# Stores of keys and values issued by ScalarE instead of SyncE, and an earlier first sample, in a two-layer cross-attention kernel on one core

## What is computed

```
x -> q = LN(x) Wq, k = LN(ctx) Wk, v = LN(ctx) Wv     16 heads of 8 columns
     rotary turn of q and k; scores = q k^T / sqrt(8) + bias(256 x 1601)
     att = softmax(scores) v;  x = x + gated projection;  x = x + tanh feed-forward
layer 2: q = LN(x) wq + bq, k = ctx wk + bk, v = ctx wv + bv, softmax(q k^T / sqrt(8)) v, wo
         then 8 experts with a top-2 gate, weighted sum
mask: all ones (looked at by the kernel, and a second program follows if it is not)
```

## Time and profile before

| | us |
|---|---|
| median of 3 runs | 655.69 (654.56 to 656.54) |
| the profiled execution | 653.17 |
| its span in the trace | 651.4 |
| PE busy | 561.3 (86% of the span) |
| ACT busy | 431.1 (66%) |
| DVE busy | 277.1 (43%) |
| POOL busy | 142.4 (22%) |

### The profile page before, as it was taken

The page is one execution under the profiler, slowest core; times in us unless marked ns, Lnnn a source line. Parts: engine busy times, 40 slices in busy tenths (PEclk is TensorE's granted clock), DMA queues, the critical chain, the costliest instruction groups (busy, mean ns, idle before and its releaser), DMA issues.

```text
span 651.4 us, 15145 instructions
## 1 busy us (share of the span) xinstructions
PE 561.3 (86%) x6326; PEld 278.2 (43%) x6326; DVE 277.1 (43%) x711; ACT 431.1 (66%) x486; POOL 142.4 (22%) x149
## 2 busy tenths in 40 slices
PE   4665896999979996999999999999999999999643
PEld 3432453545434553445555445434443443443231
DVE  5732742483754424544242243134344343433333
ACT  1224554866747773777778897998789869888400
POOL 5552622354436003541011000100000000000000
PEclk9867997999979997999999999999999999999856
DMA  6366264438755700445370066039016501000000
GB/s 166 94 186 178 71 218 168 104 115 243 226 157 146 264 26 5 138 130 179 83 189 28 27 147 141 27 82 230 4 46 144 133 10 53 2 1 10 1 0 12
DMA packets 54185, 68.12 MB, mean 105 GB/s; under 512 B 13347, under 2 KB 45551, under 8 KB 54112
## 3 DMA queue, kind: packets, MB, share of 16 engines
q1 hardware_dynamic: 50528, 59.29, 32.8%
q0 software_dynamic: 1280, 6.56, 3.4%
q10 hardware_dynamic: 2304, 1.25, 0.7%
HBM read 35.20 MB, written 18.83 MB: 83 GB/s over the span
## 4 chain that ended last, share of the span: by engine, by line
PE 53%; issue 14%; ACT 10%; SPq 7%; DMA 7%; DVE 7%; POOL 1%; ACTq 0%; POOLq 0%; DVEq 0%
PE ps L430 19%; PE ps L414 10%; ACT probs L941 8%; PE ps L408 7%; DMA k_scratch<-k_parts 4%; PE ps L360 4%; SPq L676 2%; PE ps L545 2%; SPq L699 1%; DMA ctx_tokens<-in_ctx 1%; PE ps L352 1%; PE ps L479 1%; PE ps L466 1%; DMA mask_q<-in_mask 1%; PE ps L472 1%
## 5 line engine op out<-in xcount | busy, mean ns | idle before, releaser
L941 ACT ACTIVATE probs<-ps 124x1024 f32<-124x1024 f32 (+1 forms) x416 | 399.8, 1024 | 110.7 <-PE ps L414 109.0
L430 PE MATMUL ps<-probs,values 124*9 124x256 f32 (+1 forms) x3328 | 221.4, 384 | 1.4 <-DVE out_sums L1268 1.3
L414 PE MATMUL ps<-q_side,k_side 63*124 63x256 bf16 (+1 forms) x1664 | 164.5, 283 | 13.0 <-ACT probs L941 11.2
L414 PEld LDWEIGHTS ps<-q_side,k_side 63*124 63x124 bf16 (+1 forms) x1664 | 98.1, 133 | 88.4 <-ACT probs L941 58.7
L430 PEld LDWEIGHTS ps<-probs,values 124*9 124x9 f32 (+1 forms) x3328 | 71.0, 90 | 94.1 <-issue 40.5
L408 PE MATMUL ps<-bias_g,bias_w 64*124 64x512 bf16 (+1 forms) x416 | 88.0, 419 | 25.5 <-ACT probs L941 22.0
L408 PEld LDWEIGHTS ps<-bias_g,bias_w 64*124 64x124 bf16 (+1 forms) x416 | 28.1, 131 | 69.3 <-ACT probs L941 45.3
L870 POOL TENSOR_TENSOR post_rstd<-post_rstd,power 128x2 f32<-128x2 f32 x12 | 8.4, 704 | 167.0 <-DVE post_rstd L1316 167.0
L967 ACT ACTIVATE k<-ps,columns_sb 128x496 f32<-128x496 f32 (+2 forms) x16 | 9.5, 594 | 48.2 <-PE ps L354 30.4
L1188 DVE SCALAR_TENSOR_TENSOR k_swapped<-ps,beta_products,k_sin_sb 32x496 f32<-32x496 f32 (+2 forms) x64 | 40.4, 631 | 0.9
L829 POOL DMA_DIRECT2D mask_q<-in_mask x16 | 9.1, 570 | 141.4 <-DVE checks L1247 141.4
(11 more groups left out here) (190 smaller groups left out, 481.6 us busy)
## 6 DMA issues: line engine op xcount, KB each, us to landing
k_side<-k_scratch SPq DMA_DIRECT2D x24, 400.2 KB, 9.0
k_side<-k_parts SPq DMA_DIRECT2D x48, 124.0 KB, 2.4
k_scratch<-k_parts SPq DMA_DIRECT2D x16, 372.0 KB, 4.1
v_scratch<-values SPq DMA_DIRECT2D x4, 936.0 KB, 8.1
values<-v_scratch SPq DMA_DIRECT2D x4, 936.0 KB, 14.4
...
```

What stands on the lines that cost most here:

```text
L414: last = pe.matmul(ps[0:width, bank, SQ * i:SQ * (i + 1)], kst[rows, j % 2, 2 * g + i, at], qst[rows, j % 2, 2 * g + i, :], start=not bias ...
L430: last = pe.matmul(ps[32 * i:32 * i + VC, ACC + g // 2, SQ * (g % 2):SQ * (g % 2) + SQ], v[0:rows, j % 2, t, h, :], p[0:rows, u % 4, SQ * ...
L941: act.activation(p[0:rows, u % 4, :], ps[0:rows, s:s + 2, :].rearrange("p a n -> p (a n)"), ACT.Exp)\
```

## The change

- The 52 stores of `store_keys` leave SP's list. ACT issues them, each right behind an exponential: layer 2's values ten units behind the slot of the chunk's keys (for the last chunk with the batch's layer 1 values), layer 2's keys eleven, layer 1's keys twelve. The stores of chunks 0 and 1 of batch 0 stand behind units 2, 3, 4 and 5, 6, 7.
- Batch 0's chunks 2 and 3 of keys move from slots 0 and 6 to slots 2 and 8, and the queries of batches 1 to 3 by one to three slots.
- The tokens of batch 0's chunks 2 and 3 are loaded by POOL; the tokens of chunk 1 move to the second place in SP's list.
- The first sample goes to banks 0 to 3, ahead of the last value product of chunk 1 and of the spreads of chunks 2 and 3, which follow the first two units' scores.
- On SP, tables and bias of the later tiles stand ahead of the second chunk's keys; the reciprocal deviations are loaded before the turned context.
- query_parts(0) stands behind the keys of batch 3's first two chunks, on DVE and on POOL.

```diff
@@ keys_at @@
-        first = {0: (0, 2), 6: (0, 3), 23: (1, 0), 27: (1, 1), 40: (1, 2), 46: (1, 3)}
+        first = {2: (0, 2), 8: (0, 3), 23: (1, 0), 27: (1, 1), 40: (1, 2), 46: (1, 3)}
...
-SPREAD_X_AT = ((0, 11), (0, 14))
-QUERIES_AT = ((0, 13), (0, 16))
+SPREAD_X_AT = ((0, 14), (0, 17))
+QUERIES_AT = ((0, 15), (0, 18))
...
-CENTRE_X_AT = ((0, 18), (0, 20))
+CENTRE_X_AT = ((0, 19), (0, 21))
@@ tensor: sample @@
-                for bank in (LOW, HIGH):
-                    fill(bank, "sample", j, c)
+                if j == 0:
+                    pe.wait_ge(qa_scaled, 3)
+                else:
+                    for bank in (LOW, HIGH):
+                        fill(bank, "sample", j, c)
...
-                    for half, bank in enumerate((LOW, HIGH)):
+                    for half, bank in enumerate((2 * c, 2 * c + 1) if j == 0 else (LOW, HIGH)):
@@ tensor: start @@
-            for k in range(KEY_STEPS[1]):
+            for k in range(2):
                 keys(0, 1, k)
-            pe.wait_ge(rs_ready, 3)
-            pe.wait_ge(qa_scaled, 3)
-            for n in (2, 3):
-                spread_rstd(n, n).then_inc(r_spread, 1)
             for c in range(2):
                 sample(0, c)
             turn_maxima(0)
+            keys(0, 1, 2)
             for u in range(2):
-
-                pe.wait_ge(cn_ready, 3 + u)
                 scores(u)
+
+            pe.wait_ge(rs_ready, 3)
+            for n in (2, 3):
+                pe.wait_ge(cn_ready, n - 1)
+                spread_rstd(n + 2, n).then_inc(r_spread, 1)
+            pe.wait_ge(cn_ready, 4)
@@ sync @@
-            load_tokens(0)
+            for n in range(2):
+                load_tokens(n)
...
             place_keys(0, 0)
-            place_keys(0, 1)
-            load_shift(0)
             load_bias(1)
             load_tables(2)
+            place_keys(0, 1, (0, 1))
+            load_shift(0)
+            place_keys(0, 1, (2,))
...
-            store_keys(0, 0)
-            store_keys(0, 1)
...
             store_rstd(1)
+            load_rstd_tiles(1)
             place_keys(0, 3)
-            load_rstd_tiles(1)
+            load_rstd(1)
             load_turned(1)
-            load_rstd(1)
             load_token_rows(2)
-            store_keys(0, 2)
-            store_keys(0, 3)
...
@@ gpsimd @@
             ones_of_keys(0, 0, H8 // 2)
+            for n in (2, 3):
+                load_tokens(n)
             power_of(*CHUNKS[1])
...
+            parts(0, 1)
             power_of(CHUNKS[2][0], KT)
-            parts(0, 1)
...
                     parts(b, n)
+                    if b == NB - 1 and n == 1:
+                        query_parts(0)
...
-                    query_parts(b - 2)
+            query_parts(1)
@@ scalar @@
+            def store_keys(b, n, step):
+                c, s = NC * b + n, n % 2
+                (t0, t1), (k_0, k_1) = CHUNKS[n], CHUNK_KEYS[n]
+                if step == 0:
+                    bank, _ = last_values(n)
+                    act.wait_ge(seen[bank], side.of(bank, "v", b, n))
+                    act.dma_start(G["v_dram"][1, b, :, t0:t1], v1s[:, s, 0:t1 - t0]).then_inc(v1_out[s], 16)
+                    if n == NC - 1:
+                        act.dma_start(G["v_dram"][0, b], v[:, b % 2]).then_inc(v0_out, 16)
+                elif step == 1:
+                    act.wait_ge(lo1, c + 1)
+                    act.dma_start(G["k_dram"][1, b, :, :, k_0:k_1], kp1[:, s, :, 0:k_1 - k_0]).then_inc(k1_out[s], 16)
+                else:
+                    act.wait_ge(lo0, c + 1)
+                    act.dma_start(G["k_dram"][0, b, :, :, k_0:k_1], kp0[:, s, :, 0:k_1 - k_0]).then_inc(k0_out[s], 16)
...
+                for step in range(3):
+                    key = {2 + step: (0, 0), 5 + step: (0, 1)}.get(u) or keys_at(*divmod(u - 10 - step, UB))
+                    if key is not None and (len(key) == 2 or key[2] == 0):
+                        store_keys(*key[:2], step)
@@ vector @@
+            norm_context(1)
             both_values(0, 0, 0)
-            norm_context(1)
             low_queries(0)
+            rotate_keys(0, 1)
+            for c in range(2):
+                sample_maxima(0, c)
+            make_shift(0)
             token_stats(2)
             token_stats(3)
             deviations(CHUNKS[2][0], KT)
-            rotate_keys(0, 1)
...
-            for c in range(2):
-                sample_maxima(0, c)
-            make_shift(0)
...
                 finish(j - 1)
+                keys(j + 1, 0)
+                keys(j + 1, 1)
                 if j > 1:
                     query_parts(j - 2)
-                keys(j + 1, 0)
-                keys(j + 1, 1)
```

69 lines of the change are left out of this document (30 added, 39 removed).

## The result

The changed kernel takes 636.53 us (median of 4 runs, 634.73 to 637.00) against 655.82 for the kernel before (4 runs). The ratio is 0.9703, with a 95% interval of 0.9678 to 0.9728: 19.3 us less. The forecast was 629 in a range of 621 to 647, so the direction and the range held, and the time is 7.5 us above the value forecast. The profiled executions are 653.17 and 636.97 us, 16.2 apart, and the rest of this text works with these two.

A forecast was written before the change was run, and what follows sets the result against it. PE was taken as the bound, losing time to four stalls in passes 0 to 2, their slow clock, and the start. Terms -3 -8 -6 -5 -7 +2 = -27 us gave 629 us (628.7 for the median), range 621 to 647.

The forecast's parts named there:

- Start, -3: Start of the kernel: the sample no longer waits for spreads, first scores at 34.4 and unit 2's at 41.6 us; -3 us.
- the tokens of chunk 1 ... come earlier: Start: chunk 1's tokens, for which DVE waited 5.99 us, come earlier; only 0.3 us of it counted.
- The token loads that POOL now issues ...: nothing: Start: POOL's token issues stand ahead of a step that waits for chunk 1's statistics anyway, so they cost nothing.
- Batch 0's chunk 2, -8: Pass 0, copy of layer 2's keys: the 7.08 us PE gap and slow clock behind it nearly all go; -8 us.
- SP has sent its large loads well before by then: Batch 0's chunk 2: ground for taking the store's landing near 2.94 us, not 8.00, where 4 us would be lost.
- engines, not queue: Rival: stores land as slowly as before where loads are under way; 7 us less gain, 636 us; chance 0.15.
- Batch 1's chunk 0, -6: Near 102 us: store issued twelve units ahead removes PE's 5.03 us wait and 1 us of slow clock; -6 us.
- Batch 2's chunk 2, -5: Near 182 us: store issued two units ahead removes PE's 3.37 us wait and 1.7 of slow clock; -5 us.
- query_parts, -7: Near 246 us: POOL's norm of batch 3 runs earlier, removing PE's 5.66 us wait and 1.3 of slow clock; -7 us.
- ACT's issues, +2: ACT issuing 52 stores: issues run hidden beside exponentials, sticking out only where two stand together; +2 us.
- My bound of 20 us above: ACT's store issues: upper bound on their cost if nothing overlapped with activations; 20 us.
- The "slower" rival: Rival: full DMA queues hold up ACT's issues at every batch's end, stopping all exponentials; 675 us; chance 0.04.

The follow-up runs named there:

- Experiment 2: The changed kernel with SP's load of chunk 1's tokens put back behind the first tables, as in the kernel before; 632.94 us.
- Experiment 12: The changed kernel with SP's load of a batch's token rows (123 partitions) issued as one of 112 and one of 11; 631.25 us.
- Experiment 7: The changed kernel with SP's next loads held until the first store of layer 2's keys has landed; 639.81 us in one run, only its trace used.
- Experiment 1: The changed kernel with ACT converting the high part of the later queries one exponential earlier, behind 21 instead of 22; 631.45 us.
- Experiment 4: The kernel before with the move of query_parts alone, on DVE and POOL; 646.87 us.
- Experiment 9: The changed kernel with each of ACT's 52 stores issued as two of half the partitions, 104 issues of the same bytes; 656.32 us.

## Why the prediction was right in sign and too large

By its own steps, in the profiled executions:

- **Start, -3: it came out at +3.4.** The reorder itself gives what was forecast once the load is out of the way, as Experiment 2's 34.37 and 41.39 us show against 34.4 and 41.6, but part of this is luck: the shift was ready 1.7 us earlier than the sum had it (29.95 against 31.7), and the way from there to the first scores took 4.4 us against the 2.7 taken, since SP's list was still at the keys of chunk 1. The step that failed is "the tokens of chunk 1 ... come earlier". They did, by 0.4 us (12.05 against 12.42), as booked; what it left out is what was put behind them. SP's list passed chunk 1's tokens over x's tokens; these had been read at once at 5.01 us and were now read at 10.71. "The token loads that POOL now issues ...: nothing" failed with it, since POOL no longer waited for chunk 1's statistics.
- **Batch 0's chunk 2, -8: -3.9 by unit 12**, some 1 us of it value products that now stand behind that mark. The residual wait was bounded by 0 and 4 us and taken near 0; PE's is 3.89 us. The failed ground is "SP has sent its large loads well before by then": sent they were, at 40.70 us, but the DMA share says that some three engines worked on one of them until 56, and splitting that load alone takes the wait away (Experiment 12). The rival "engines, not queue" was the right mechanism here, with 4 us of stall and 1 of clock left, -3. Experiment 7 shows it from both sides (2.5 and 17.87 us). The Trainium skill's rule, page "DMA: Bandwidth & Descriptors", section "Issuing engines are not separate DMA queues", holds in this case. What the move to ACT gives is the choice of when to issue, not a faster landing.
- **Units 12 to 24, nothing booked: +4.0 (-2.9 up to unit 16, then +6.8).** The two parts alone mislead, since 3.1 us of PE's work crossed the mark between them. PE's wait of 1.55 us for DVE's `v` in the kernel before (at 75.77 us) is gone, which is a gain not booked. The loss is one conversion. The change moves `high_queries` from 5 to 4 exponentials behind the second query slot while that slot itself moves by 2, and I followed the stores only. Experiment 1 gives back 4.4 us for that line, and with it the stretch takes 24.5 us against 24.9 in the kernel before. That comparison is of single executions, which differ by up to 3 us in this stretch (Experiment 4).
- **Batch 1's chunk 0, -6: -6.8. Batch 2's chunk 2, -5: -5.4. query_parts, -7: -7.2**, and Experiment 4 finds the last alone. Here the sizes came from a gap on PE and the slow rows behind it, and both held. For batch 2's chunk 2 the landing was taken as 2.94 us and was 5.55; the copy waited 1.55 us for it, but PE did not.
- **ACT's issues, +2: 0.** The row that showed an issue beside an activation was the right one, for single issues. My bound of 20 us above was not idle either: Experiment 9 reaches 17 us with the double number. The "slower" rival was not far away; by Experiment 9 it needs two issues together, and above all the hold-up at a batch's end.

The sum: -27, with +6.4 for the start, +4.1 for chunk 2, -2.9 and +6.8 for the stretches up to units 16 and 24, -0.8, -0.4 and -0.2 for the three that gave more, -2 for the issues and -0.2 in the last passes, is -16.2 us, the table's -16.1 but for rounding. That the measured 636.5 us are what the rival "engines, not queue" gave (636) is chance: its stall at chunk 2 came true, but its losses at batches 2 and 3 did not, and what went wrong at the start and with the conversion, some 11 us, is in no term of it. Of the signs named beforehand, these did not come: the copy of chunk 2 waited 4.72 us and not under 4, that of batch 2's chunk 2 waited too, first scores stood at 41.12 us and unit 2's at 48.13. Batch 3's keys without the 5.66 us, the last passes unchanged and no exponential behind an issue came as named.
